# Slot filings of the last tiles on GpSimd: their place and their waits changed, in a fused attention and mixture-of-experts kernel

## The chip, the cores and the metric

One core of one Trainium2 chip runs the whole program. The metric is the device time of one execution in microseconds. The kernel before took 1765.45 us, the median of three runs (1762.36, 1765.45 and 1768.41 us).

## The reference, cut to what matters

The input is 16 batches of 1024 tokens of 512 numbers. It goes through a cross-attention block and then through a feed-forward block with 32 experts:

```python
x = x + _L0_xattn_ref(_layernorm(x), ctx, Wq, Wk, Wv, Wo, bo)      # 8 heads, 64 context rows
h = _layernorm(x)
logits = X @ gate_w.T;  scores = sigmoid(logits)
idx = top_k(scores + bias, 4);  w = scores[idx] / sum(scores[idx])
pos = cumsum(onehot(idx)) - 1;  valid = pos < C                    # C = 512 rows an expert
xe[eid, pos] = X;  ye = (silu(xe @ W1) * (xe @ W3)) @ W2           # an expert at a time
x = x + sum(ye[eid, pos] * w) + silu(X @ sw1.T) * (X @ sw3.T) @ sw2.T
```

A token goes to four experts, and its row in an expert's list (its slot) is a running count over all tokens before it. So the last tokens' slots have to be known before any expert's list is complete.

## The kernel before, in words

**Two stages.** The token stage works on 128 tiles of 128 tokens, in groups of four tiles (32 groups, numbers 0 to 31). The expert stage follows: 32 experts (e = 0 to 31), each with four chunks of 128 rows.

**The token stage** is a software pipeline. In step n the engines work on different tiles at fixed lags: `scores` (L485, TensorE) on tile n-8, `mix` (L500) on tile n-10, `logits` (L517) on tile n-14, and for every fourth step the shared feed-forward (`up_half` L527, `down_tile` L537) and `rank` (L548 to L554), which counts a group's tokens by expert. VectorE turns ranks to slots (`slot_over` L1189 to `slot_list` L1211 and L1212, which raises `slots_ready`). `TAIL` is 137: the steps 0 to 136 are in the loop, and what is left of the last tiles is written out by hand behind it on each engine. In this tail TensorE runs, in order: `mix(127)`, `logits(123)`, the first half of `last_up` of group 30, `logits(124)`, `rank(30)`, `logits(125)`, the second half of `last_up(30)`, `logits(126)`, `logits(127)`, `last_down(30)`, `rank(31)`, and then the shared feed-forward of group 31. ScalarE's `route_exp` (L868) starts the routing of a group: it waits for `logits_done`, the semaphore that TensorE raises with the last matmul of each tile's logits. The names `BUT_ONE`, `LAST` and `FINAL` are group 30, group 31 and tile 127.

**Slot filing.** GpSimd writes each token's number into the table of its slots with an indirect DMA (`file`, L923): one for each of a tile's four choices, so four filings a tile and 16 a group, 512 in all. In the loop, step n files tile n-20, between two subtractions and a multiplication of softmax probabilities (`prob`, L947). In step 135 the order is the other way round: first the multiplication for tile 127, then the four filings of tile 115. Step 136 files tile 116 once group 29's slots are there, and a loop behind the steps files tiles 117, 118 and 119. The groups 30 and 31 are filed choice by choice instead (`file_slot`, L985: four filings, one for each tile of the group):

- `file_last(0)`, before the first gather: choices 0 and 1 of group 30, a wait for group 31's slots, choices 0 and 1 of group 31;
- `file_last(2)`, before the gather of expert 2: choice 2 of both groups and choice 3 of group 30;
- `file_last(3)`, before the gather of expert 3: choice 3 of group 31.

**From the table to the experts.** `experts_sync` on SyncE waits, for each choice q, until all eight `file_slot` filings of that choice have landed (`filed[q]`), and loads a piece of the table into `idx_near`: expert 0's rows for q = 0, expert 1's for q = 1, expert 2's for q = 2, experts 3 to 11 for q = 3. `gather(e)` on GpSimd (L1545, four indirect DMAs) waits for that load and brings the expert's rows. For the experts 0 and 1 nothing else stands in GpSimd's queue between `file_last(0)` and their gathers.

**The expert stage** is a pipeline of steps as well. In its step n TensorE turns the rows of expert n (`turn`, L1606), multiplies up expert n-1 (`up`, L1580, in two halves of 16 matmuls) and down expert n-2 (`down`, L1620). Of step 2 the order is: first half of `up(1)`, first part of `down(0)`, `turn(2, 0)`, and so on. `turn(e, 0)` waits for all four gathers of expert e, for expert 0 chunk by chunk. `t_done` and `ue_done` are the semaphores that TensorE raises with each turned chunk and with each half of an expert's up product.

The waits are few in the code of GpSimd; a semaphore increment `passed` follows each, which nothing waits for.

Of the kernel before, what the change touches and what calls it, by code (L numbers as in the profile page):

```python
# [36 lines left out]
E, TOP, CAP, I = 32, 4, 512, 256  # L37
TOKENS = B * S
TILES = TOKENS // P
GROUPS = TILES // 4  # L40
# [18 lines left out]
X_LOAD, LN1_SUM, LN1_SQUARE, ROOTS, XT_LOAD, XT_SPLIT, SCORES, MIX, X1 = 2, 3, 4, 6, 6, 7, 8, 9, 10  # L59
X2, LOGITS, FFN_UP, FFN_DOWN = 13, 14, 17, 19  # L60
ROUTE, MEMBERS, SLOTS_AT, WEIGHTS, OUT, W_STORE, TABLE = 17, 18, 19, 20, 20, 21, 20
STEPS = TILES - 4 + TABLE + 4
NEWTON = 7
LAST, BUT_ONE = GROUPS - 1, GROUPS - 2
FINAL = TILES - 1
TAIL = TILES + X1 - 1
LATER = 3
WEIGHTS_AT = (126, 128, 131, 133)


def at(n, lag):

    t = n - lag
    return t if 0 <= t < TILES else None
# [60 lines left out]
def tokens_and_experts(nc, x, xT, ctxT, wqT, wk, wv, wo, bo, gateT, bias, w1, w3, w2, sw1T, sw3T, sw2T, out, x2aug, table):  # L135
    stack = ExitStack()
    with stack:
# [123 lines left out]
        scores_done, p_turned, o_done = sem("scores_done"), sem("p_turned"), sem("o_done")  # L261
        x2_turned, logits_done = sem("x2_turned"), sem("logits_done")
# [20 lines left out]
        counted, rank_done, rank_read = sem("counted"), sem("rank_done"), sem("rank_read")  # L283
# [4 lines left out]
        passed = sem("passed")  # L288
# [50 lines left out]
        with nc.Block() as block:  # L339
# [570 lines left out]
            @block.gpsimd  # L910
            def _(pool):
                def file(t, first, end):
                    if t is None:
                        return
                    g, i = t // 4, t % 4
                    if i == 0 and first == 0:
                        if g == 0:
                            pool.wait_ge(fill_stored, (2 * PAD // P + 1) * 16)
                            pool.wait_ge(const_set, 11)
                        pool.wait_ge(slots_ready, 2 * g + 2)  # L920
                        pool.sem_inc(passed, 1)
                    for q in range(first, end):
                        pool.indirect_dma_start(  # L923
                            table, bass.IndirectOffsetOnAxis(ap=slot[:, g % 2, i, q:q + 1], axis=0),
                            tok_line[:, g % 2, i, :], None, bounds_check=SLOTS - 1, oob_is_err=False).then_inc(scattered[g % 2], 16)

                def step(n):
                    t = at(n, XT_SPLIT)
                    if t is not None:
                        pool.wait_ge(xt_hi, t + 1)  # L930
                        after(pool, scores_done, t - 1)
                        pool.tensor_tensor(xt_l[:, t % 2, :, :], xt[:, t % 2, :, :], xt_h[:, t % 2, :, :].bitcast(F32),  # L932
                                           ALU.subtract).then_inc(xt_lo, 1)
                    for c in range(2):
                        g = group_at(n, FFN_UP + c + 1)
                        if g is not None:
                            pool.wait_ge(ht_hi, g * 2 + c + 1)
                            after(pool, g_done, g * 4)
                            after(pool, u_done, g * 4)
                            pool.tensor_tensor(ht_l[:, c, :], hid[:, :], ht_h[:, c, :].bitcast(F32),  # L940
                                               ALU.subtract).then_inc(ht_lo, 1)
                    if n != FINAL + SCORES:
                        file(at(n, TABLE), 0, TOP)
                    t = at(n, SCORES)
                    if t is not None:
                        pool.wait_ge(rsum_done, t + 1)
                        pool.tensor_tensor(prob[:, t % 2, :, :], prob[:, t % 2, :, :],  # L947
                                           rsum[:, :].unsqueeze(2).to_broadcast([P, H, SKV]), ALU.mult).then_inc(prob_done, 1)
                    if n == FINAL + SCORES:
                        file(at(n, TABLE), 0, TOP)  # L950

                pool.memset(zrow, 0.0).then_inc(zero_set, 1)
                pool.memset(kbd[:, :, :, :], 0.0).then_inc(zero_set, 1)
                pool.memset(ident[:, :], 0.0).then_inc(ident_set, 1)
                pool.wait_ge(ident_set, 1)
                pool.affine_select(out=ident[:, :], in_=ident[:, :], compare_op=ALU.not_equal, fill=1.0,
                                   base=0, pattern=[[-1, P]], channel_multiplier=1).then_inc(ident_set, 1)

                pool.iota(fill.rearrange("p (e c l) -> p e c l", e=E, l=LINE), [[0, E], [1, CAP // P], [0, LINE]], base=TOKENS,
                          channel_multiplier=CAP // P).then_inc(zero_set, 1)  # L960
                pool.memset(earlier[:, :], 0.0).then_inc(const_set, 1)
                pool.wait_ge(const_set, 1)

                pool.affine_select(out=earlier[:, :], in_=earlier[:, :], compare_op=ALU.is_ge, fill=1.0,
                                   base=0, pattern=[[-1, P]], channel_multiplier=1).then_inc(const_set, 1)
                pool.memset(ones[:, :], 1.0).then_inc(const_set, 1)
                pool.memset(first_slot[:, :], -TOPSLOT).then_inc(const_set, 1)
                pool.wait_ge(const_set, 4)
                pool.iota(first_slot[0:1, :], [[CAP, E]], base=0, channel_multiplier=0,
                          allow_small_or_imprecise_dtypes=True).then_inc(const_set, 1)  # L970
                pool.memset(before[:, :], 0.0).then_inc(const_set, 1)
                pool.memset(guess_bias[:, :], GUESS_BIAS).then_inc(const_set, 1)
                pool.memset(ones_f[:, :], 1.0).then_inc(const_set, 1)
                pool.memset(bo_max[:, :], 0.0).then_inc(const_set, 1)
                pool.iota(end_slot[:, :], [[CAP, E]], base=int(CAP - TOPSLOT), channel_multiplier=0,
                          allow_small_or_imprecise_dtypes=True).then_inc(const_set, 1)
                pool.iota(tok[:, :], [[P, TILES]], base=0, channel_multiplier=1).then_inc(const_set, 1)
                for n in range(TAIL):
                    step(n)
                for t in range(TAIL - TABLE, 4 * BUT_ONE):  # L980
                    file(t, 0, TOP)

                def file_slot(g, q):
                    for i in range(4):
                        pool.indirect_dma_start(  # L985
                            table, bass.IndirectOffsetOnAxis(ap=slot[:, g % 2, i, q:q + 1], axis=0),
                            tok_line[:, g % 2, i, :], None, bounds_check=SLOTS - 1, oob_is_err=False).then_inc(filed[q], 16)

                def file_last(part):
                    if part == 0:  # L990
                        pool.wait_ge(slots_ready, 2 * BUT_ONE + 2)
                        pool.sem_inc(passed, 1)
                        file_slot(BUT_ONE, 0)
                        file_slot(BUT_ONE, 1)
                        pool.wait_ge(slots_ready, 2 * LAST + 2)
                        pool.sem_inc(passed, 1)
                        file_slot(LAST, 0)
                        file_slot(LAST, 1)
                        pool.wait_ge(o_done, TILES)
                        for r in range(2):  # L1000
                            pool.wait_ge(x2_stored[r], TILES // 2 * 16)
                            pool.wait_ge(w_stored[r], GROUPS // 2 * 16)
                    elif part == 2:
                        file_slot(BUT_ONE, 2)
                        file_slot(LAST, 2)
                        file_slot(BUT_ONE, 3)
                    elif part == 3:
                        file_slot(LAST, 3)

                experts_gpsimd(pool, file_last, [(out_stored[r][k], len(range(r, GROUPS, XRING)) * 16)  # L1010
                                                 for r in range(XRING) for k in range(2)])

# [415 lines left out]
CHUNKS = CAP // P  # L1428
# [13 lines left out]
def experts(nc, stack, ident, w1, w3, w2, out, x2aug, table):  # L1442
# [38 lines left out]
    passed = sem("passed")  # L1481
# [45 lines left out]
    def experts_gpsimd(pool, file_last, out_stored):  # L1527
# [34 lines left out]
        def step(at):  # L1562
            e = at(SCATTER)
            if e is not None:
                scatter(e)
            e = at(GATHER)
            if e is not None:
                if e in (2, 3):
                    file_last(e)
                gather(e)  # L1570

        file_last(0)
# [226 lines left out]
```

## Time and profile before

| | us |
|---|---|
| median of three runs (lowest, highest) | 1765.45 (1762.36, 1768.41) |
| span of the profiled execution, first to last instruction | 1810.0 |
| TensorE busy in it (matmuls) | 1641.8 (91%) |
| VectorE, ScalarE, GpSimd busy | 1378.9, 1066.3, 1252.4 |
| mean granted TensorE clock | 0.964 |

Of the profiled execution the span is the only time that is given; what lies around it is not told. It is 44.6 us longer than the median of the runs without a profile. Times in the trace count from the first instruction. "Remote" behind a wait, or "another core or an unknown queue" in the chain, means that the wait ended by a semaphore whose update the profile could not put down to an instruction that had just ended. With one core there is no other core. Matmul records can be missing, and so can the updates that they made.

### The profile page before, as it was taken

What the parts mean: (1) busy time and instruction counts of PE and PEld (TensorE: products, weight loads), DVE (VectorE), ACT (ScalarE), POOL (GpSimd) and SP (SyncE); (2) the same over time, 40 slices, a digit from 0 to 9 for tenths busy, and PEclk for the clock granted to TensorE, in tenths of its full rate; (3) what the DMA queues carried; (4) which work ended last, traced back from release to release, by engine and by line L of the source; (5) the groups of instructions that cost most, each with busy time, mean ns of one, the idle gap of its engine ahead of it and who ended that gap; (6) DMA issues with size and microseconds to landing.
All of it is one profiled execution on the core that took longest, in us unless ns stands there. A gap on an engine that the chain in (4) does not pass through costs nothing.

```text
span 1810.0 us, 31933 instructions
## 1 busy us (share of the span) xinstructions
PE 1641.8 (91%) x9056; PEld 1023.7 (57%) x9056; DVE 1378.9 (76%) x3486; ACT 1066.3 (59%) x2368; POOL 1252.4 (69%) x1104
## 2 busy tenths in 40 slices
PE   6999999999999999999999999999447999999991
PEld 4565656666566665656666565655224555555550
DVE  4678988987898897889779789898425777777771
ACT  4777766776776676777767767765213444444440
POOL 2337777777777777777767677777475787777874
PEclk8999999999999999999999999999678999999996
DMA  7557876667776666677666577777249889988665
GB/s 247 144 135 166 193 163 151 174 155 154 181 183 152 162 168 155 174 167 178 164 149 170 152 182 171 161 191 170 61 142 264 139 172 166 208 190 167 103 85 79
DMA packets 474532, 293.75 MB, mean 162 GB/s; under 512 B 342643, under 2 KB 385397, under 8 KB 474356
## 3 DMA queue, kind: packets, MB, share of 16 engines
q1 hardware_dynamic: 429300, 239.03, 51.9%
q0 software_dynamic: 45056, 52.67, 18.5%
q8 instruction: 74, 1.21, 0.3%
q14 instruction: 102, 0.84, 0.2%
HBM read 135.06 MB, written 110.17 MB: 135 GB/s over the span
## 4 chain that ended last, share of the span: by engine, by line
PE 45%; issue 17%; DVE 16%; ACT 9%; another core or an unknown queue 4%; DMA 3%; POOL 2%; SPq 2%; DVEq 0%; ACTq 0%; POOLq 0%
PE O_ps L500 9%; PE S_ps L485 8%; PE GE_ps L1580 5%; PE UE_ps L1580 4%; PE G_ps L527 4%; PE YE_ps L1620 4%; PE U_ps L527 3%; PE PREP_ps L583 2%; POOL out L1557 2%; PE PREP_ps L566 2%; DVE top_s L1280 2%; DVE x_l L1221 1%; DMA pt_l<-p_l 1%; PE TE_ps L1606 1%
## 5 line engine op out<-in xcount | busy, mean ns | idle before, releaser
L923 POOL DMA_INDIRECT slot_table<-tok_line,slot x480 | 507.7, 1058 | 132.0 <-issue 128.1
L932 POOL TENSOR_TENSOR xt_l<-xt,xt_h 128x512 fp32r<-128x512 f32 x128 | 164.6, 1286 | 179.5 <-ACT xt_h L758 179.5
L799 ACT ACTIVATE prob<-S_ps,rs 128x512 f32<-128x512 f32 x128 | 88.0, 688 | 257.3 <-DVE S_ps L1286 166.5
L485 PE MATMUL S_ps<-a_h,xt_h 128*128 128x512 f32 x512 | 213.3, 417 | 2.4 <-DVE m_l L1259 2.4
L500 PE MATMUL O_ps<-m_h,pt_h 128*128 128x512 f16 x512 | 195.9, 383 | 20.0 <-DMA pt_l<-p_l 18.9
L485 PE MATMUL S_ps<-a_h,xt_l 128*128 128x512 f32 x512 | 202.1, 395 | 0.0
L485 PE MATMUL S_ps<-a_l,xt_h 128*128 128x512 f32 x512 | 202.0, 395 | 0.0
L500 PE MATMUL O_ps<-m_h,pt_l 128*128 128x512 f16 x512 | 194.7, 380 | 0.0
L500 PE MATMUL O_ps<-m_l,pt_h 128*128 128x512 f16 x512 | 194.6, 380 | 0.0
L947 POOL TENSOR_TENSOR prob<-prob,rsum 128x512 f32<-128x512 f32 x128 | 135.4, 1058 | 83.0 <-DVE rsum L1314 62.3
L1557 POOL DMA_INDIRECT out<-ye,idx_far x80 | 126.3, 1579 | 52.2 <-issue 27.7
L485 PEld LDWEIGHTS S_ps<-a_h,xt_h 128*128 128x128 f32 x512 | 98.1, 192 | 37.4 <-issue 16.1
L1672 ACT ACTIVATE xe_h<-TE_ps 128x512 f16<-128x512 f32 x128 | 75.8, 593 | 67.7 <-PE TE_ps L1606 51.6
L1654 ACT ACTIVATE the<-GE_ps 128x512 f32<-128x512 f32 x64 | 38.2, 597 | 126.7 <-PE GE_ps L1580 90.5
L1221 DVE TENSOR_TENSOR x_l<-x,x_h 128x512 f16<-128x512 f32 x126 | 86.4, 685 | 33.4 <-ACT x_h L858 26.7
L1620 PE MATMUL YE_ps<-down_w,he_h 128*128 128x512 f32 x256 | 110.8, 433 | 0.6 <-DVE he_l L1712 0.6
L485 PEld LDWEIGHTS S_ps<-a_h,xt_l 128*128 128x128 f32 x512 | 97.5, 190 | 21.9
L500 PEld LDWEIGHTS O_ps<-m_h,pt_h 128*128 128x128 f16 x512 | 49.9, 97 | 102.9 <-issue 29.5
L485 PEld LDWEIGHTS S_ps<-a_l,xt_h 128*128 128x128 f32 x512 | 98.0, 191 | 17.3
L1606 PE MATMUL TE_ps<-ident_r,rows 128*128 128x128 f32 x512 | 67.2, 256 | 43.9 <-DVE xe_l L1718 34.1
L846 ACT ACTIVATE x<-xr,nb,rs 128x512 f32<-128x512 f32 x128 | 102.8, 803 | 1.0 <-DVE nb L1045 1.0
L1700 DVE SCALAR_TENSOR_TENSOR gte<-the,GE_ps 128x512 f32<-128x512 f32 x64 | 44.0, 688 | 77.5 <-ACT the L1654 49.8
(245 smaller groups left out, 4848.8 us busy)
## 6 DMA issues: line engine op xcount, KB each, us to landing
xt<-in_xT SPq DMA_DIRECT2D x128, 256.0 KB
xr<-in_x SPq DMA_DIRECT2D x64, 512.0 KB, 3.8
x2aug<-x SPq DMA_DIRECT2D x128, 256.0 KB
out<-xr SPq DMA_DIRECT2D x64, 512.0 KB, 3.2
up_more<-in_w SPq DMA_DIRECT2D x36, 256.0 KB
slot_table<-tok_line,slot POOLq DMA_INDIRECT x512
up_w<-in_w SPq DMA_DIRECT2D x28, 256.0 KB
down_more<-in_w SPq DMA_DIRECT2D x18, 256.0 KB
```

The source lines that it names most:

```text
L485: last = pe.matmul(S_ps[t % 2][:, :], left[:, kc, :], right[:, b % 2, kc, :], start=(m == 0), stop=(m == 3 * KD - 1))
L500: last = pe.matmul(O_ps[:, :], left[:, t % 2, p, :], right[:, b % 2, p, :], start=(m == 0), stop=(m == 3 * PAIRS - 1))
L527: last = pe.matmul(bank[:, :], up_sb[:, kc, w0 + c * P:w0 + (c + 1) * P], part[:, g % 2, kc, :], start=(m == 0), stop=(m == 2 * KD - 1))
L799: act.activation(prob[:, t % 2, :, :], S_ps[t % 2][:, :].rearrange("p (h j) -> p h j", h=H), ACT.Exp, scale=rs[:, q % 2, 0, t % 2:t % 2 + ...
L846: act.activation(x2[:, t % 2, :], x_tile(t), ACT.Identity, bias=nb2[:, q % 2, t % 2:t % 2 + 1], scale=rs[:, (q + LATER) % 2, 1, t % 2:t % ...
L923: pool.indirect_dma_start(table, bass.IndirectOffsetOnAxis(ap=slot[:, g % 2, i, q:q + 1], axis=0), tok_line[:, g % 2, i, :], None, bounds_ ...
L932: pool.tensor_tensor(xt_l[:, t % 2, :, :], xt[:, t % 2, :, :], xt_h[:, t % 2, :, :].bitcast(F32), ALU.subtract).then_inc(xt_lo, 1)
L947: pool.tensor_tensor(prob[:, t % 2, :, :], prob[:, t % 2, :, :], rsum[:, :].unsqueeze(2).to_broadcast([P, H, SKV]), ALU.mult).then_inc(pro ...
L1221: dve.tensor_tensor(split_rows(t)[1][:, :], x2[:, t % 2, :], split_rows(t)[0][:, :], ALU.subtract).then_inc(x2_lo, 1)
L1557: pool.indirect_dma_start(out, bass.IndirectOffsetOnAxis(ap=index(e, c), axis=0), ye[:, e % 4, c, :], None, bounds_check=TOKENS + PAD - 1, ...
L1580: last = pe.matmul(bank[:, :], up_set(e)[:, kc, w0 + c * P:w0 + (c + 1) * P], part[:, e % TURNED, kc, :], start=(n == 0), stop=(n == 2 * K ...
L1620: last = pe.matmul(YE_ps[i % 2][:, :], part[:, e % 2, c, i * P:(i + 1) * P], down_w[:, e % 2, c, :], start=(n == 0), stop=(n == 2 * KI - 1))
```

## The change

`HELD` is 136. Of the filings in the token stage, those of tile 115 (step 135) now stand before the multiplication of tile 127's probabilities. Tile 116 is no longer filed in step 136. Behind the loop each of the tiles 116 to 119 has its own wait on a semaphore of TensorE: the last mix and the logits of tile 123; the rank of group 30; the logits of tile 126; the logits of tile 127. A fifth wait, for the rank of group 31, stands before `file_last(0)`. In `file_last(2)` two waits are added: for the fourth turned chunk of expert 0, before choice 2 of group 30, and for both halves of expert 0's up product, before choice 2 of group 31 and choice 3 of group 30. The number of filings is the same, and no other engine's program is touched.

```diff
+HELD = TAIL - 1
...
-                    if n != FINAL + SCORES:
+                    if n < HELD:
                         file(at(n, TABLE), 0, TOP)
                     t = at(n, SCORES)
...
-                    if n == FINAL + SCORES:
-                        file(at(n, TABLE), 0, TOP)
...
                 for n in range(TAIL):
                     step(n)
-                for t in range(TAIL - TABLE, 4 * BUT_ONE):
-                    file(t, 0, TOP)
+                pool.wait_ge(o_done, TILES)
+                pool.wait_ge(logits_done, FINAL - 3)
+                pool.sem_inc(passed, 1)
+                file(HELD - TABLE, 0, TOP)
+                pool.wait_ge(rank_done, GROUPS - 1)
+                pool.sem_inc(passed, 1)
+                file(HELD - TABLE + 1, 0, TOP)
+                pool.wait_ge(logits_done, FINAL)
+                pool.sem_inc(passed, 1)
+                file(HELD - TABLE + 2, 0, TOP)
+                pool.wait_ge(logits_done, TILES)
+                pool.sem_inc(passed, 1)
+                file(HELD - TABLE + 3, 0, TOP)
+                pool.wait_ge(rank_done, GROUPS)
+                pool.sem_inc(passed, 1)
...
-                def file_last(part):
+                def file_last(part, turned_done=None, up_done=None):
...
                     elif part == 2:
+                        pool.wait_ge(turned_done, CHUNKS)
+                        pool.sem_inc(passed, 1)
                         file_slot(BUT_ONE, 2)
+                        pool.wait_ge(up_done, 2)
+                        pool.sem_inc(passed, 1)
                         file_slot(LAST, 2)
                         file_slot(BUT_ONE, 3)
...
-                    file_last(e)
+                    file_last(e, t_done, ue_done)
```

## Rows read from the trace of the kernel before

**Rows 1.** The page of the profile: its head

```profile
span 1810.0 us, 31933 instructions
```

**Rows 2.** Windows: us; busy (x) of PE, PEld, DVE, ACT, POOL; PEclk; DMA share, GB/s

```profile
1250.00:1300.00 50.00, 24.29 (x132) 11.70 (x130) 23.38 (x81) 15.15 (x31) 25.44 (x27) 0.73 0.35 76
1300.00:1350.00 50.00, 29.58 (x118) 17.73 (x118) 19.78 (x55) 6.22 (x13) 31.42 (x33) 0.73 0.42 128
1350.00:1400.00 50.00, 31.77 (x159) 18.52 (x160) 24.41 (x37) 16.11 (x26) 28.83 (x26) 0.83 0.91 249
```

**Rows 3.** Timeline of ScalarE: start us, us, instruction, [idle before <-releaser]

```profile
1267.38 0.63 ACT L858 ACTIVATE p_h<-x 128x512 f16<-128x512 f32 x1
1285.04 0.28 ACT L868 ACTIVATE lexp<-R_ps 128x128 f32<-128x128 f32 x1 [17.03 <-remote]
...
1339.18 0.60 ACT L1672 ACTIVATE xe_h<-TE_ps 128x512 f16<-128x512 f32 x1 [2.23 <-remote]
```

**Rows 4.** Timeline of TensorE in the tail of the token stage

```profile
1266.17 0.18 PE L517 MATMUL R_ps<-gate_sb,x2t_l 128*128 128x32 bf16 x1
...
1300.38 0.18 PE L517 MATMUL R_ps<-gate_sb,x2t_l 128*128 128x32 bf16 x1
...
1309.28 0.23 PE L548 MATMUL R_ps<-member,earlier 128*128 128x128 bf16 x1 [0.84 <-DVE member L1165]
```

**Rows 5.** Timeline of GpSimd, 1240 to 1300 us

```profile
1254.64 1.04 POOL L947 TENSOR_TENSOR prob<-prob,rsum 128x512 f32<-128x512 f32 x1 [4.38 <-DVE rsum L1314]
1255.84 1.01 POOL L923 DMA_INDIRECT slot_table<-tok_line,slot  x1 [0.15 <-issue]
...
1280.52 0.97 POOL L923 DMA_INDIRECT slot_table<-tok_line,slot  x1 [0.30 <-issue]
1294.51 0.97 POOL L985 DMA_INDIRECT slot_table<-tok_line,slot  x1 [13.03 <-DVE slot L1212]
```

**Rows 6.** Timeline of GpSimd, 1300 to 1370 us

```profile
1303.77 0.97 POOL L985 DMA_INDIRECT slot_table<-tok_line,slot  x1 [0.30 <-issue]
1312.71 0.97 POOL L985 DMA_INDIRECT slot_table<-tok_line,slot  x1 [7.96 <-DVE slot L1212]
...
1322.99 1.04 POOL L1545 DMA_INDIRECT rows<-x2aug,idx_near  x1 [0.39 <-issue]
...
1349.93 1.04 POOL L1545 DMA_INDIRECT rows<-x2aug,idx_near  x1 [0.30 <-issue]
...
1359.11 0.97 POOL L985 DMA_INDIRECT slot_table<-tok_line,slot  x1 [0.30 <-issue]
1365.50 1.05 POOL L1545 DMA_INDIRECT rows<-x2aug,idx_near  x1 [5.42 <-DMA idx_near<-slot_table]
```

**Rows 7.** Who waited for whom in the whole span: us in total, times, longest

```profile
ACT lexp L868 <- remote: 21.8, 2, 17.0
DVE xr L1116 <- remote: 18.5, 12, 2.2
```

**Rows 8.** Timeline of TensorE at the start of the expert stage

```profile
1329.50 1.23 PE L1606 MATMUL TE_ps<-ident_r,rows 128*128 128x128 f32 x8 [3.43 <-issue]
...
1346.20 0.38 PE L1580 MATMUL UE_ps<-xe_l,up_w 128*128 128x512 f16 x1
...
1370.82 0.38 PE L1580 MATMUL UE_ps<-xe_l,up_w 128*128 128x512 f16 x1
...
1377.48 0.46 PE L1606 MATMUL TE_ps<-ident_r,rows 128*128 128x128 f32 x4
...
1390.30 0.46 PE L1606 MATMUL TE_ps<-ident_r,rows 128*128 128x128 f32 x4
```

**Rows 9.** The chain that ended last: start us, us, what

```profile
1348.38 14.09 another core or an unknown queue
1362.49 0.70 DVE hie L1708
```

**Rows 10.** DMA issues on the page: size of one, median us to landing

```profile
xr<-in_x SPq DMA_DIRECT2D x64, 512.0 KB, 3.8
```

## The prediction

> **What bounds the kernel now.** The windows come first: between 1250 and 1350 us TensorE is busy for only 24.3 and 29.6 of 50 us and its granted clock falls to 0.73, and between 1350 and 1400 us to 31.8 of 50 [rows 2]. This is the seam between the two stages. The chain that ended last has two long pieces in it that wait for something the profile can't name; one is 14.1 us long [rows 9], the other is ScalarE's wait of 17.0 us [rows 3]. The timelines give both sides of each. TensorE's last logits matmul of tile 123 ended at 1266.35 us [rows 4]. ScalarE was free at 1268.0 us, and its `route_exp`, which waits for that matmul's semaphore and for one of VectorE that is older still, started at 1285.04 us, 17.0 us later [rows 3]. Meanwhile GpSimd issued filings without a break: 20 of them, from 1255.84 to 1281.49 us [rows 5]. The second piece lies the same way: TensorE finished the first half of expert 0's up product at 1346.58 us [rows 8], VectorE's product of it started at 1362.49 us [rows 9], and the last of a row of filings and gathers ended at 1360.08 us [rows 6].
>
> My reading is that a semaphore update of TensorE can be held while filings follow each other closely, and comes up to four us after they end. In the pipeline, where only four filings stand together, the same sign is small: VectorE's residual waited for such an update 12 times, at most 2.2 us [rows 7]. A smaller case of the tail is the logits of tile 127: they ended at 1300.56 us [rows 4], and `route_exp` of group 31 waited until a run of eight filings was over, at 1304.74 us [rows 6]; that is the other 4.8 of the 21.8 us of ScalarE's waits [rows 7].
>
> The profile names none of this as caused by filings. **By the Trainium skill** (PSUM — Partial Sum Buffer, Engine vs sequencer instructions) an update attached to a matmul fires when the instruction completes. By that rule the 17.0 us would have been none, and a filing could hold nothing up; the trace does not agree here, and the rule's own outcome is the rival on the other side below.
>
> **The change, part by part**, as the profiled execution would show it.
>
> *Tile 115 before the multiplication.* GpSimd waited 4.38 us before that multiplication, to 1254.64 us [rows 5]. A filing takes 1.28 us (eight of them filled the 10.28 us from 1312.71 us to the first gather, [rows 6]), four take 5.1 us, so the multiplication comes 5.1 - 4.4 = 0.7 us later; a residual's update may be held in that time, by up to the 2.2 us of rows 7. The last mix has some slack behind it. Bounds 0 and 2 us; I take +0.5.
>
> *The run of twenty, now four by four.* Tile 116 starts when the logits of tile 123 are known, 1266.4 us, so nothing is in the way of that update. `route_exp(30)` starts at 1268.0 instead of 1285.0: **-17.0 us** for all that follows it, the slots of group 30, the rows of the last tiles and their logits. Tile 116's filings end at 1271.5 us; rank 30 comes about 5 us behind its `route_exp`, as rank 31 did (1304.7 to 1309.3 us), near 1273 us and so after them. Tile 117 follows it. Tiles 118 and 119 follow the logits of tiles 126 and 127, which I take to be a few us apart at most, less than four filings; so they make one run of eight, about 1282 to 1292 us.
>
> *Rank 31.* Before, TensorE was through with `down` at 1308.44 us and the rank started 0.84 us later, when routing was through [rows 4]. Routing starts earlier now (its update falls in the first 2 us of a run), so the rank is tied to the `down` product: -0.8. Its own update falls late in the run of eight, like the held one at 1300.56 us: +1.2, between 0 and the 4.2 us of that case. With the 0.5, rank 31 is known at 1309.9 - 17.0 - 0.8 + 1.2 + 0.5 = 1293.8 us.
>
> *Choices 0 and 1 of group 30 behind rank 31.* These eight filings ran from 1294.51 us [rows 5] in time that nothing else wanted. Behind the new wait they stand ahead of group 31's eight. Before, the first gather started at 1322.99 us [rows 6], 13.1 us after rank 31; now it is 0.3 + 16 x 1.28 + 0.4 = 21.1 us after it: **+8.0 us**. First gather at 1314.9 us, 8.1 us earlier than before. SyncE's load of the first table piece waits for the same filings and just fits.
>
> *The run of sixteen, and the shared feed-forward of group 31.* Its products are now under filings from the first. Before, the run from 1312.71 us did not hold them. Cost 0 if so again; if one is held to the end of the run, TensorE is through some 5 us after the first rows have landed: 0 to +5, I take 0 as the trace shows.
>
> *`file_last(2)`.* From the first gather on, before: first turn +6.5, last turned chunk known +16.2 [rows 3], first turn of expert 2 at +54.5 and of expert 3 at +67.3 (1377.48 and 1390.30, [rows 8]). Now, with GpSimd waiting: last chunk at +14.2 (two of the 16.2 are held updates, as the 2.23 us of rows 3). The first half of up was through 7.4 us after the last chunk was known (1339.18 to 1346.58); the stall is gone; from VectorE's product to the end of the second half it took 1371.20 - 1362.49 = 8.7 us, with 1 us before it: 14.2 + 7.4 + 1 + 8.7 = +31.3. Then eight filings, 10.2 us, in which the table piece comes in after the first four: gather of expert 2 from +41.5, its fourth piece issued 3.9 us on and landed 5.0 later. That landing is between 3.8, a plain load [rows 10], and 6.5, the first gather's; I take the middle. First turn of expert 2: +50.4. Choice 3 of group 31 ends at 41.5 + 5.2 + 5.1 = +51.8; from there to the gather of expert 3 it was 5.4 us (1360.08 to 1365.50, [rows 6]): +57.2, landed +66.1. One step of the expert stage is 12.8 us [rows 8], so turning could go at 50.4 + 12.8 = +63.2; it waits for the rows, +66.1 against +67.3 before: **-1.2**. What is late next is thus gather 3. So the stall of 14.1 us is mostly paid back, as waits of TensorE for gathers 2 and 3.
>
> **Sum**: -8.1 - 1.2 = -9.3 us. The rest of the expert stage is the same work. The sum is against the profiled span, 1810.0 us [rows 1], which is 44.6 us above the median of the runs; carried over whole it gives 1765.45 - 9.3 = 1756.1 us. Low and high ends of the unknowns (0 and 2; 0 and 4.2; 0 and 5; landing ± 1.3; and, as TensorE idles less, some of its clock of 0.73 back in this stretch, up to 3) give 1749 to 1762.
>
> **The rivals.**
>
> *Only the profiled execution stalls.* This ends on the other side. The profiled span is 45 us above the runs, while its matmuls run at full clock nearly everywhere else, and the two stalls and the 4.2 us are 36 us. If TensorE's updates come at once in the timed runs, GpSimd is the bound of the seam: before, its 20, 8 and 8 filings would stand end to end. The change then puts eight filings behind rank 31 for nothing (21.1 against 13.1: +8), and `file_last(2)` waits for what was no hindrance: before, gather 2 went 27 us after the first gather (1349.9 against 1323.0, [rows 6]) and gather 3 would follow at 42.5; now they go at about +37.5 and +53.2, and turning expert 3 goes from +50.5 to +61.3: +10.8. Together +19: **1784 us**. It decides as soon as less than about half of each stall is real. For it: the 45 us. Against it: ScalarE, VectorE and the DMAs show no such lag in the same execution. Chance 0.29.
>
> *Half real.* -8 in the first stall, little in the second: between -4 and +8, 1765 to 1771 us. Chance 0.12.
>
> *The run of sixteen holds.* The new run is twice as long as the one it replaces, and the feed-forward of group 31 lies under it: +5 on the forecast, and more if two updates are held: 1761 to 1764 us, no difference that can be told. For it: 1300.56 us; against it: the run from 1312.71 us. Chance 0.10.
>
> *It does not break the stall.* If the wait at 1268 us has another cause, such as loading of code, it stays, and the waits cost their 8 us: 1773 us. Chance 0.04.
>
> **How the numbers follow.** My forecast has 0.45, its own range is 1749 to 1762 us. What a measurement of this kernel can tell from no change is 0.3%, 5.3 us. Of the forecast's case 0.38 is beyond that and 0.07 within it; half real gives 0.02 faster, 0.04 same, 0.06 slower; the held run gives 0.02 faster and 0.08 same; the other two are slower. Faster 0.42, same 0.19, slower 0.39. The range, 1748 to 1785 us, reaches from the low end of the forecast over all rivals: both signs hold much of the chance.
>
> **What would show it.** Right: `route_exp(30)` within 2 us of 1268 us, and no wait over 5 us that ends remote; 16 filings in one run after rank 31; the first gather near 1315 us; TensorE waiting for the gathers of experts 2 and 3. Wrong: if the profiled span falls by 9 us or so while the runs get slower, the stall belongs to the profile. If the product of group 31 ends after 1320 us, the run of sixteen held it. If a new wait of 10 us or more ends remote inside the four-filing runs, my reading of what holds the updates is wrong.

## The result: 0.97% slower, while the profiled span fell by 33 us

The changed kernel takes 1779.98 us (median of four runs, 1778.97 to 1783.31). The kernel before, run beside it, takes 1763.9 us (four runs, 1760.04 to 1768.41). The ratio is 1.0097, 95% interval 1.0081 to 1.0113, or +17.1 us (14.3 to 19.9); the two medians differ by 16.1 us. Of all 70 executions of the kernel before with a time on record, 69 lie between 1757.96 and 1770.66 us, and one, at a granted clock of 0.65, took 2374.55 us. None is near the 1810.0 us that the profile of before had as its span. The forecast of 1756.1 us was wrong; the rival "only the profiled execution stalls" said 1784 us, 19 more than before, and that is close to what happened.

### The profile after

Head and first part of the page of the changed kernel:

```profile
span 1777.2 us, 31940 instructions
...
PE 1636.8 (92%) x9056; PEld 1021.2 (57%) x9056; DVE 1379.4 (78%) x3486; ACT 1066.5 (60%) x2368; POOL 1255.8 (71%) x1104
```

This execution took 1778.97 us by the device's clock, 1.8 us more than its span. The span of before was 1810.0 us [rows 1] against runs of 1765. So the profiles say -33 us and the runs say +16. That points at the profile of before as one that doesn't describe the kernel before.

Windows of the changed kernel, columns as in rows 2:

```profile
1250.00:1300.00 50.00, 26.05 (x131) 14.52 (x129) 27.82 (x97) 10.04 (x20) 34.02 (x36) 0.82 0.40 112
1300.00:1350.00 50.00, 29.25 (x134) 16.40 (x135) 18.51 (x28) 12.92 (x22) 27.47 (x28) 0.77 0.41 113
1350.00:1400.00 50.00, 45.10 (x241) 27.52 (x240) 34.12 (x52) 21.17 (x34) 37.92 (x30) 1.00 1.02 264
```

TensorE idles here about as much as in rows 2, and then runs at full clock from 1350 us. But before the right thing to compare with exists (the experiments), these rows prove nothing.

Timeline of ScalarE, the `route_exp` of group 30 and that of group 31:

```profile
1248.69 0.26 ACT L869 ACTIVATE lexp<-R_ps 128x128 f32<-128x128 f32 x1
...
1264.01 0.26 ACT L869 ACTIVATE lexp<-R_ps 128x128 f32<-128x128 f32 x1
```

No wait stands before either, where there were 17.0 us before that of group 30 [rows 3]. TensorE's last matmul for the logits of tile 123 ended at 1247.12 us, that for tile 127 at 1263.91 us, so the two started 1.6 and 0.1 us behind what they wait for. In the whole span there is not one wait that ends remote, where rows 7 had 21.8 and 18.5 us of them. With the 0.1 us of group 31, the trace now agrees with the rule that the prediction cited: by the Trainium skill (PSUM — Partial Sum Buffer, Engine vs sequencer instructions) an update attached to a matmul fires when it completes.

Timeline of GpSimd in the changed kernel:

```profile
1228.55 1.06 POOL L948 TENSOR_TENSOR prob<-prob,rsum 128x512 f32<-128x512 f32 x1
...
1236.55 1.06 POOL L948 TENSOR_TENSOR prob<-prob,rsum 128x512 f32<-128x512 f32 x1
1248.06 1.00 POOL L924 DMA_INDIRECT slot_table<-tok_line,slot  x1 [10.44 <-PE R_ps L518]
1255.18 0.97 POOL L924 DMA_INDIRECT slot_table<-tok_line,slot  x1 [2.27 <-PE R_ps L555]
1263.76 0.97 POOL L924 DMA_INDIRECT slot_table<-tok_line,slot  x1 [3.65 <-PE R_ps L518]
...
1274.11 0.97 POOL L997 DMA_INDIRECT slot_table<-tok_line,slot  x1 [0.30 <-issue]
...
1294.56 1.05 POOL L1561 DMA_INDIRECT rows<-x2aug,idx_near  x1 [0.30 <-issue]
...
1305.99 1.01 POOL L997 DMA_INDIRECT slot_table<-tok_line,slot  x1 [1.24 <-PE TE_ps L1622]
...
1319.38 0.97 POOL L997 DMA_INDIRECT slot_table<-tok_line,slot  x1 [8.53 <-PE UE_ps L1596]
...
1329.59 1.04 POOL L1561 DMA_INDIRECT rows<-x2aug,idx_near  x1 [0.30 <-issue]
...
1345.18 1.04 POOL L1561 DMA_INDIRECT rows<-x2aug,idx_near  x1 [5.44 <-DMA idx_near<-slot_table]
```

GpSimd now stands idle at five of the new waits: 10.4 us before tile 116, 2.3 before tile 117, 3.7 before tile 118, and in the last run 1.2 and 8.5 us. At the wait for rank 31 it does not: it came there at 1274.1 us, and the rank had ended before that (first row of the next fence). TensorE pays with waits for rows:

```profile
1271.23 0.23 PE L555 MATMUL R_ps<-before,ones 128*128 128x128 bf16 x1
...
1298.16 0.72 PE L1622 MATMUL TE_ps<-ident_r,rows 128*128 128x128 f32 x4 [10.13 <-DMA rows<-x2aug,idx_near]
...
1337.52 0.75 PE L1622 MATMUL TE_ps<-ident_r,rows 128*128 128x128 f32 x4 [12.55 <-DMA rows<-x2aug,idx_near]
...
1355.52 0.54 PE L1622 MATMUL TE_ps<-ident_r,rows 128*128 128x128 f32 x4 [2.99 <-DMA rows<-x2aug,idx_near]
```

### The profile page after: what moved, and what is told of

It is laid out like the page before. It is cut to its first block and busy times, and to the rows that moved or that the text cites. A ratio compares the mean times of both kernels' runs of the same rounds, so it can differ in the third digit from the quotient of the medians.

```text
span 1777.2 us, 31940 instructions
## 1 busy us (share of the span) xinstructions
PE 1636.8 (92%) x9056; PEld 1021.2 (57%) x9056; DVE 1379.4 (78%) x3486; ACT 1066.5 (60%) x2368; POOL 1255.8 (71%) x1104
## 5 line engine op out<-in xcount | busy, mean ns | idle before, releaser
L1734 DVE TENSOR_TENSOR xe_l<-TE_ps,xe_h 128x512 f16<-128x512 f32 x128 | 87.8, 688 | 42.6 <-ACT xe_h L1688 40.8
L486 PEld LDWEIGHTS S_ps<-a_l,xt_h 128*128 128x128 f32 x512 | 97.1, 190 | 17.1
L1745 DVE TENSOR_SCALAR ye<-YE_ps,rows 128x512 f32<-128x512 f32 x128 | 95.5, 746 | 11.9 <-PE YE_ps L1636 10.0
```

The costliest lines, as they stand in the source:

```text
L486: last = pe.matmul(S_ps[t % 2][:, :], left[:, kc, :], right[:, b % 2, kc, :], start=(m == 0), stop=(m == 3 * KD - 1))
L1734: dve.tensor_tensor(xe_l[dst], TE_ps[i % 2][:, :].rearrange("p (c t) -> p c t", c=KD), xe_h[dst], ALU.subtract).then_inc(t_lo, 1)
L1745: dve.tensor_scalar(ye[:, e % 4, i, :], YE_ps[i % 2][:, :], w, None, ALU.mult).then_inc(y_read, 1)
```

## The experiments

Two theories. **Q**: in ordinary executions TensorE's updates come at once. What bounds the seam is GpSimd's queue, whose filings and gathers stand end to end; time in which it waits makes TensorE's rows late. The holds of 17 and 14 us belonged to one execution. **H**: the holds are in every run, and something else makes the change slow.

### The kernel before, profiled again

> The kernel before, unchanged, with a profile of its own. Theory Q (queue): the holds of TensorE's updates belonged to the one profiled execution; in ordinary ones they come at once and GpSimd's filings stand end to end and bound the seam. It expects a span near 1762 us, within 5 us of the timed runs, no wait over 3 us that ends remote, the multiplication of tile 127's probabilities near 1237 us as in the changed kernel, 36 filings without a real pause and the first gather near 1284 us, 10 us before the changed kernel's 1294.6. Theory H (held): updates are held in ordinary runs too, and the loss of the change comes from elsewhere. It expects holds of 10 us or more again and a span over 1790 us. Time by both: ratio 1.000.

1764.86 us, ratio 1.0 (0.9987 to 1.0012). Span 1766.6 us, its execution 1768.37 us. Its timeline of GpSimd and of TensorE, and its windows beside those of rows 2:

```profile
1228.78 1.07 POOL L947 TENSOR_TENSOR prob<-prob,rsum 128x512 f32<-128x512 f32 x1
...
1235.69 1.04 POOL L947 TENSOR_TENSOR prob<-prob,rsum 128x512 f32<-128x512 f32 x1 [4.37 <-DVE rsum L1314]
1236.89 1.01 POOL L923 DMA_INDIRECT slot_table<-tok_line,slot  x1 [0.15 <-issue]
...
1283.84 1.04 POOL L1545 DMA_INDIRECT rows<-x2aug,idx_near  x1 [0.30 <-issue]
...
1310.40 1.04 POOL L1545 DMA_INDIRECT rows<-x2aug,idx_near  x1 [0.30 <-issue]
...
1328.08 1.05 POOL L1545 DMA_INDIRECT rows<-x2aug,idx_near  x1 [7.19 <-DMA idx_near<-slot_table]
```

```profile
1287.45 0.51 PE L1606 MATMUL TE_ps<-ident_r,rows 128*128 128x128 f32 x4 [3.31 <-DMA rows<-x2aug,idx_near]
...
1318.28 0.75 PE L1606 MATMUL TE_ps<-ident_r,rows 128*128 128x128 f32 x4 [3.62 <-DMA rows<-x2aug,idx_near]
...
1338.41 0.75 PE L1606 MATMUL TE_ps<-ident_r,rows 128*128 128x128 f32 x4 [5.60 <-DMA rows<-x2aug,idx_near]
```

```profile
1250.00:1300.00 50.00, 30.87 (x151) 17.37 (x152) 29.32 (x97) 12.37 (x24) 37.82 (x38) 0.80 0.53 156
1300.00:1350.00 50.00, 36.95 (x174) 21.68 (x173) 25.40 (x38) 16.20 (x27) 33.78 (x31) 0.86 0.66 172
1350.00:1400.00 50.00, 47.68 (x254) 29.35 (x252) 36.09 (x56) 22.26 (x36) 35.86 (x28) 1.00 0.87 202
```

Its execution lies within the range of the timed runs: this is the kernel before as it runs. No wait ends remote. From 1236.89 to 1283.84 us 36 filings stand end to end, 47 us, or 1.30 us each (the prediction had 1.28). Group 31's slots were written at 1269.90 us, 3.7 us before the last eight of them began, so here the queue is late and not the slots. Before the first turns of experts 0, 2 and 3 TensorE waits only 3.3, 3.6 and 5.6 us for rows. Against these windows, and not against rows 2, the change takes TensorE from 30.9 to 26.1 and from 37.0 to 29.3 us of busy time, 12.5 us of idle more by 1350 us.

The profile of before was already late when the seam began: the multiplication for tile 127 stands at 1254.64 us there [rows 5] and at 1235.69 us here. Windows over the same stretch of the token stage, the first line from the profile of before, the second from this one:

```profile
100.00:1200.00 1100.00, 1076.83 (x6149) 676.26 (x6148) 939.42 (x2639) 777.29 (x1829) 798.94 (x723) 1.00 0.69 167
```

```profile
100.00:1200.00 1100.00, 1092.32 (x6249) 686.92 (x6248) 957.87 (x2693) 791.33 (x1860) 813.16 (x735) 1.00 0.72 170
```

In the disturbed execution each engine got 1.4 to 1.9% less busy time into the same 1100 us, at full granted clock, and the seam began 19 us late. Of the 43.4 us by which its span is longer than this one, 18.9 were lost ahead of GpSimd's multiplication for tile 126, 33.0 from there to the first turn of expert 3, and 8.5 were won back behind it. The prediction gave 36 of its 45 us to the seam's holds and did not look at the stretch ahead of it.

Two more profiles of the kernel before and one more of the changed one:

> The kernel before, unchanged, profiled again. Theory Q (the holds of TensorE's updates belonged to one execution, not to the kernel): no wait over 1 us that ends remote, the profiled span within 3 us of the execution's time, near 1765 us, the last eight filings and the first gather end to end. Theory H (holds recur whenever it is profiled long enough): a span over 1790 us with ScalarE or VectorE waiting over 10 us for a finished matmul.

> The same once more, as for the run before it: theory Q a span near 1765 us without holds, theory H a span over 1790 us with them.

> The changed kernel, unchanged, profiled again. Theory Q: span near 1777 us, GpSimd idle some 10, 2 and 4 us before tiles 116 to 118, 0.3 us at the wait for rank 31 and 8 to 9 us at the wait for the up product, with the first gather about 66 us after the multiplication of tile 126's probabilities. Theory H: holds, and a span over 1790 us.

Executions of 1764.71, 1763.97 and 1779.19 us, with spans of 1762.9, 1762.2 and 1777.4 us, and no remote wait in any. As theory Q said, with two sizes off: the first gather of the changed kernel comes 64.5 and not 66 us behind the multiplication, and the wait for the up product is 11.4 and not 8 to 9 us. The wait before tile 118 was 2.6 us, where some 4 were expected. Who waited for whom there, columns as in rows 7:

```profile
POOL slot_table L924 <- PE R_ps L518: 11.9, 2, 9.3
POOL slot_table L997 <- PE UE_ps L1596: 11.4, 1, 11.4
```

The experiments below and the profile after make twelve later profiles in all, and none shows a wait that ends remote. Theory H has fallen. Why the first profile had such waits is open; they did not come again.

### A common scale

The executions reach the seam some 4 us apart. So the table counts, in us, from a mark: the start of GpSimd's multiplication for tile 126 in each profile (the first row of the two timelines of GpSimd above). Columns: first gather, gather of expert 2, gather of expert 3, TensorE's `turn(3, 0)`, then the measured ratio with its interval.

| kernel | gather 0 | gather 2 | gather 3 | turn(3, 0) | ratio |
|---|---|---|---|---|---|
| before | 55.1 | 81.6 | 99.3 | 109.6 | 1.0 |
| only the wait for rank 31 | 61.5 | 87.9 | 104.3 | 115.2 | 1.0030 (1.0016, 1.0045) |
| only the two waits of the last run | 55.2 | 91.0 | 106.6 | 117.8 | 1.0052 (1.0034, 1.0071) |
| only the wait for the up product | 56.1 | 94.7 | 110.3 | 120.6 | 1.0050 (1.0034, 1.0065) |
| only the tail | 65.7 | 91.9 | 107.4 | 118.2 | 1.0049 (1.0030, 1.0068) |
| the tail without the wait for rank 31 | 66.5 | 92.8 | 108.4 | 119.8 | 1.0035 (1.0022, 1.0047) |
| the whole change | 66.0 | 101.0 | 116.6 | 127.0 | 1.0097 (1.0081, 1.0113) |
| only the order of tile 115 | 54.4 | 82.4 | 98.2 | 109.3 | 0.9991 (0.9980, 1.0002) |
| order, and choice 2 of group 30 moved up | 57.0 | 77.8 | 93.6 | 104.3 | 0.9975 (0.9962, 0.9988) |

Each row is one profile. The first gather of the kernel before came at 55.1 to 55.2 in all three of its later profiles, gathers 2 and 3 at 81.6 to 82.7 and 98.3 to 99.3, and turn(3, 0) at 109.3 to 110.3. The second profile of the whole change had 64.5, 101.6, 117.2 and 127.7. So differences of 1 us say nothing here, and for the first gather behind the new waits not even 1.5 us do.

The shift of turn(3, 0) is not the whole account of the time. From there to the end of the span it was 424.3 to 428.2 us in the three later profiles of before, and 421.7 us in both of the changed kernel. A part of the delay is won back in the expert stage; among other things TensorE waited less for the rows of the experts from 12 on, 2.2 and 2.5 us in all against 4.6 to 6.9. From the mark to the end of the span it was 533.6 to 537.8 us before and 548.7 and 549.4 us after.

### The two halves of the change

The tail alone (the diff of the change without the two waits in `file_last(2)`):

> Only the first part of the change: tile 115 before the multiplication, the four waits for tiles 116 to 119 and the wait for rank 31; no waits in the last run. Q: GpSimd idles while it waits (10.4 + 2.3 + 3.7 us in the changed kernel, against 10.2 us or less that it can catch up nowhere), so the first gather stays near 1294.6 us, 10 us late; gathers 2 and 3 follow at the old distance of 27 and 42.5 us, so about +9 us in time (+7 to +11). H: the run of twenty is broken, so -5 us or better, and the loss must be in the last run.

1772.8 us, +8.6 us by the ratio (5.3 to 12.0).

```profile
1248.37 1.00 POOL L924 DMA_INDIRECT slot_table<-tok_line,slot  x1 [9.30 <-PE R_ps L518]
1255.49 0.97 POOL L924 DMA_INDIRECT slot_table<-tok_line,slot  x1 [2.26 <-PE R_ps L555]
1264.10 0.97 POOL L924 DMA_INDIRECT slot_table<-tok_line,slot  x1 [3.70 <-PE R_ps L518]
```

The last run alone:

```diff
+                        pool.wait_ge(turned_done, CHUNKS)
+                        pool.sem_inc(passed, 1)
                         file_slot(BUT_ONE, 2)
+                        pool.wait_ge(up_done, 2)
+                        pool.sem_inc(passed, 1)
                         file_slot(LAST, 2)
```

> Only the two waits in the last run (before choice 2 of group 30 and of group 31), the tail as in the kernel before. Q: the first gather stays at its old place, the gathers of experts 2 and 3 come 35 and 50.6 us after it as in the changed kernel instead of 27 and 42.5, so TensorE waits some 8 us longer for them: +8 us in time (+6 to +11). H: the second hold of 14 us is broken and paid back in waits for gathers: -2 to +2.

1772.19 us, +9.2 us (6.0 to 12.5).

```profile
1309.92 0.97 POOL L985 DMA_INDIRECT slot_table<-tok_line,slot  x1 [9.11 <-PE UE_ps L1584]
...
1335.69 1.05 POOL L1549 DMA_INDIRECT rows<-x2aug,idx_near  x1 [5.42 <-DMA idx_near<-slot_table]
```

8.6 and 9.2 add up to 17.8, and the whole change costs 17.1; each of the two can be off by some 3 us. That the halves add is what one queue would give in which they stand one behind the other. The tail moves the first gather by 10.6 us, and turn(3, 0) by 8.6; the two shifts of turn(3, 0), 8.6 and 8.2, lie within the intervals of the two costs.

### Which wait of the tail, which of the last run

The wait for rank 31 alone, two lines ahead of `file_last(0)`:

> Only the wait for rank 31 before the filings of group 30, nothing else changed. My prediction took this wait for the dear one of the tail (+8 us). Q: before it 20 filings end near 1263 us, rank 31 is known near 1271 us, so GpSimd idles some 8 us and the first gather comes 7 us later: +6 us in time (+4 to +8). That it cost nothing in the changed kernel, where the filings of tiles 118 and 119 cover it, does not speak against that. H: the wait stands between two runs that were apart anyway: -1 to +1.

1769.63 us, +5.3 us (2.8 to 7.9).

```profile
1270.88 0.97 POOL L987 DMA_INDIRECT slot_table<-tok_line,slot  x1 [6.24 <-PE R_ps L554]
```

Alone it costs 6.2 us of GpSimd's time, because with the filings of the tiles in one run GpSimd comes to it before the rank has ended. The tail without it:

> The kernel before with the first part of the change but without the wait for rank 31: tile 115 before the multiplication, and tiles 116 to 119 filed one by one behind the last mix and the logits of tile 123, rank 30, the logits of tile 126 and those of tile 127. Theory Q (in ordinary executions TensorE's updates come at once, and what is paid is GpSimd's idle time before these filings): the wait for rank 31 cost nothing in the kernel that had all five (0.31 us idle before it), so this is as slow as that one, 1771 to 1774 us, and the idle time before tiles 116 to 118 is 10.4, 2.3 and 3.7 us again. Rival R (the wait for rank 31, which alone cost 4.8 us, is a share of the cost here too): 1767 to 1769 us.

1770.89 us or +6.2 us (3.9 to 8.3), between the ranges of the two theories, and with an interval that overlaps that of the whole tail. The times leave it open; the traces decide what the queue did: the first gather comes at 66.5 without this wait and at 65.7 with it, and GpSimd idles 10.0, 2.3 and 3.9 us before the tiles 116 to 118. Within the change this wait adds no idle time: the waits before it have used it up. One thing does not fit: turn(3, 0) is 10.2 us later in this profile, and the kernel only 6.2 us slower.

The last run with the second wait only:

> The kernel before with only the second wait of the last run: choice 2 of group 31 and choice 3 of group 30 wait until the up product of expert 0 is complete; choice 2 of group 30 waits for nothing. Theory Q: the wait for the turned rows is met when GpSimd comes to it, so all of the 7.3 us that both waits cost is this one's: 1771 to 1774 us, one idle time of 9.1 us before the filings behind the up product. Rival: the two waits share the cost, because choice 2 of group 30 is held too: 1767 to 1770 us.

1773.24 us or +8.8 us (6.0 to 11.5), as theory Q expected: this wait alone costs as much as both, as far as can be told. GpSimd idled 11.5 us and not 9.1 here, since in this execution the up product was known 84.4 us behind the mark of the table and not 80.8; the medians of the runs, 1773.24 and 1772.19 us, don't tell the two kernels apart.

```profile
1310.57 0.97 POOL L985 DMA_INDIRECT slot_table<-tok_line,slot  x1 [11.54 <-PE UE_ps L1582]
```

### The opposite: less idle time in the queue

If GpSimd's queue is the bound, then filling its idle time should make the kernel faster. Tile 115 before the multiplication, as in the change, and nothing else:

```diff
-                    if n != FINAL + SCORES:
-                        file(at(n, TABLE), 0, TOP)
+                    file(at(n, TABLE), 0, TOP)
...
-                    if n == FINAL + SCORES:
-                        file(at(n, TABLE), 0, TOP)
```

> The kernel before with only the order of the last step turned: tile 115 is filed before the multiplication of tile 127's probabilities, into the 4.4 us in which GpSimd waited for the row sums. Theory Q: GpSimd's filings stand end to end from there to the first gather (36 of them), so they all come 4.4 us earlier; the last eight then wait 0.5 us or so for group 31's slots, known at about 1269.9 us, and the first gather goes at 1280.3 instead of 1283.8 us. TensorE waited 3.3 us for its rows, so the expert stage starts 3.3 us earlier; the multiplication comes 0.7 us later, which the last mix may pay. Together -2 to -3.5 us: 1761 to 1763 us. Theory H (GpSimd's filings are not what bounds the seam): no change, or +0.7.

1762.54 us, 0.9991 (0.9980 to 1.0002): less than expected, and no difference that can be told. Alone this run does not tell Q from H. The queue was 4.4 us ahead, but came to group 31's slots before they were there:

```profile
1269.90 0.97 POOL L982 DMA_INDIRECT slot_table<-tok_line,slot  x1 [3.21 <-DVE slot L1209]
```

Of the 4.4 us won, 3.2 are idle again, one place further on (0.5 were expected): without the gap the queue is early, and the slots bound it. The second kernel puts work there that was done later before:

```diff
                     if part == 0:
+                        file_slot(BUT_ONE, 2)
                         pool.wait_ge(slots_ready, 2 * BUT_ONE + 2)
...
                     elif part == 2:
-                        file_slot(BUT_ONE, 2)
```

> The same, and choice 2 of group 30 is filed right behind choices 0 and 1, ahead of the wait for group 31's slots, and so no more in the last run. Theory Q: the four filings take back the time won by the order before the first gather (1284.6 against 1283.8 us), but eight filings and not twelve stand between the gathers of experts 1 and 2, so the gather of expert 2 goes 4.3 us earlier (1306.1 against 1310.4) and that of expert 3 with it; TensorE's waits of 3.6 and 5.6 us for their rows shrink. First turn of expert 3 about 4 us earlier: -3 to -4 us, 1760.5 to 1762 us. Rival: the start of the expert stage decides and not the later gathers: +0.8 us.

1761.25 us, 0.9975 (0.9962 to 0.9988): -4.4 us (-6.7 to -2.1), the fastest of all versions and the only one whose interval lies below 1.

```profile
1269.60 0.97 POOL L982 DMA_INDIRECT slot_table<-tok_line,slot  x1 [0.30 <-DVE slot L1209]
...
1305.07 1.04 POOL L1542 DMA_INDIRECT rows<-x2aug,idx_near  x1 [0.30 <-issue]
...
1320.93 1.05 POOL L1542 DMA_INDIRECT rows<-x2aug,idx_near  x1 [5.61 <-DMA idx_near<-slot_table]
```

The first gather is 1.9 us later than before, the gather of expert 2 3.8 us earlier and turn(3, 0) 5.3 us earlier. TensorE's wait for the rows of expert 2 is gone, and that for expert 3 is 2.7 us. What is left there is the load of the table piece for choice 3, 5.6 us before gather 3.

## Why the prediction was wrong

**The step that failed** is the first one: that an update of TensorE can be held while filings follow each other closely. The prediction took -17.0 us from it in the run of twenty and a stall of 14.1 us in the last run, which the waits were to buy out. What the runs showed in its place: the twelve later profiles have no hold, in runs of 4, 12, 24 and 36 filings. GpSimd's queue bounds the seam, and the waits put into it made GpSimd idle for 16.4 us in the tail and 9.8 us in the last run; the kernel became 17.1 us slower. So the gain of the prediction was the repair of a fault that only the profiled execution had. The 44.6 us between span and runs were named there, and carried over whole, as though they were the same for both kernels; in all the later profiles the span is 1.8 us below its own execution's time.

**Its chance.** The rival had 0.29. Against it the prediction put that ScalarE, VectorE and the DMAs showed no such lag. That does not tell between a kernel that holds and an execution that does. The sum of the profile's own excess does: if the updates were held in every run, the 45 us stay unexplained; if in this execution alone, the holds explain most of them. (17.0, 14.1 and 4.2 us are 35.3 and not 36; against the later profile the seam was 33.0 us longer.) The prediction named the 45 us as what spoke for the rival, and gave them too little weight.

**Tile 115, +0.5.** The multiplication comes 8.0 us behind the one before it and not 7.0: +1.0, and the last mix is no later (its last matmul starts 16.6 us behind the mark of the table, against 16.8 to 16.9). No cost shows: the kernel with this order alone has a ratio of 0.9991. That it fills 4.4 us of the bounding queue was not seen.

**Rank 31 and the eight filings behind it, +8.0.** The mechanism is not the one that pays: GpSimd comes to this wait after the rank. The first gather is later all the same, by 10.9 us (66.0 against 55.1; by 9.4 in the second profile), and the idle times account for it: idle 10.4 + 2.3 + 3.7 us before the three tiles, less the 4.4 us before the multiplication and three ordinary issue times of 0.3 us, is 11.1 us. The prediction took the waits for the tiles as free, since it counted from a rank that came late.

**The run of sixteen, 0.** The size was right, since under a run of 24 filings nothing was held; but the question had come from the same false step.

**`file_last(2)`, -1.2.** The place of turn(3, 0) with the waits was about right, and the place without them, from which the cost is counted, was wrong. In the rival's case (with up done without a stall) the prediction put turn(3, 0) at 61.3 us behind the first gather, and 61.0 were measured (127.0 - 66.0), 63.2 in the second profile. But for the kernel before without stalls it said 50.5, and that is 54.5 (109.6 - 55.1), 54.1 to 55.1 over the three later profiles: gather 3 went 43.1 to 44.2 us behind the first, not 42.5, and its rows were turned 10.3 to 11.5 us after it, not 8. (The wait of 7.2 us for the table piece, shown above, was 5.5 us in the other two profiles.) So the last run cost 6.5 us behind the first gather by these two profiles, 8.1 us when it was changed alone, where the rival said 10.8. As to the forecast's -1.2, the stall of 14.1 us that the waits were to buy out was not there.

**The rival's sum** was +19 (8 + 10.8), the runs say +17.1. By the traces it is 10.9 behind the common mark and 6.5 more to turn(3, 0), 17.4 in all. The total was near in part by luck: the first term was too small, the second too large, and what the expert stage wins back behind turn(3, 0) was in neither.

**The marks of right and wrong** pointed the right way: "if the profiled span falls by 9 us or so while the runs get slower, the stall belongs to the profile". It fell by 33 and not by 9, since what was lost ahead of the seam did not come again either.

## What to carry to other kernels

Before a stall in a trace is given a price, the span of that execution is set against the runs: here 1810 against 1765 us marked a disturbed execution, and none of its waits that ended "remote" came again in three more profiles of the same kernel. If such a profile is all there is, the forecast is worked out for the kernel without the stalls first, and the stalls get a chance, not the sum. And where an engine's queue has been found to stand end to end up to the next stage's first transfer (here 36 filings), a wait put into it costs most of the idle time that it makes: 5.3 us of time for 6.2 us idle before rank 31, 9.2 for 9.1 and 8.8 for 11.5 in the last run, 8.6 and 6.2 for some 10 to 11 us net in the tail. Work moved into its idle time gains, as long as what it needs is there: the waits of this change cost 1%, and filling two gaps of the same queue gained 0.25%.

## What the runs showed of the hardware that was not expected

One profiled execution can differ from all others of the same kernel in kind: its holds of up to 17 us, and 1.4 to 1.9% less busy time of every engine in the same 1100 us at full granted clock. In four profiles of the kernel before it came once. What it was stays open.

GpSimd's pace of filing was the same however many followed each other: 36 in a row took 47 us in the kernel before (1.30 us each), 24 in a row 30.8 us in the changed one (1.28 us each).
